# One-hot columns of the key tiles shared between VectorE and ScalarE, and the decode of the sorted list ahead of the last two key products

## What is computed

```python
edge_index = jnp.stack([src, dst])                    # 50000 edges
xn = _layernorm(x, axis=-1)
x = x + gnn(xn, edge_index, w1, b1, w2, b2) \
      + mix(xn[None], Wqkv, bqkv, Wproj, bproj, temperature)[0]
x = x + ffn(_layernorm(x, axis=-1)[None], gate_w, ..., gamma, beta)[0]
# gnn: msgs = mlp(x[col]); agg = segment_sum(msgs, row); mlp(x + agg)
# mix: kn, qn are normalised rows per head (8 heads of 32);
kv_mod = einsum('bhni,bhnj,bhne->bhije', kn, kn, vN)  # all products of two key channels
kv     = einsum('bhnd,bhne->bhde', kn, vN)
```

## Time and profile before

| | us |
|---|---|
| median of 3 runs | 1569.05 |
| lowest, highest | 1567.12, 1572.82 |
| the profiled execution: its time | 1570.75 |
| the profiled execution: its span | 1569.1 |

### The profile page before, as it was taken

How to read it: one execution, slowest core, us unless ns; L and a number is a source line. 1 busy time by engine, 2 the same in 40 slices (tenths; PEclk the granted TensorE clock), 3 DMA queues, 4 the chain that set the end, 5 groups by cost and what they waited for, 6 DMA issues and landing times.

```text
span 1569.1 us, 25750 instructions
## 1 busy us (share of the span) xinstructions
PE 1142.1 (73%) x7084; PEld 777.7 (50%) x7085; DVE 969.9 (62%) x2315; ACT 407.5 (26%) x1088; POOL 953.5 (61%) x1069
## 2 busy tenths in 40 slices
PE   3888869888874776676767776676896399999900
PEld 2656534333332443444444444443685299999900
DVE  4998989999983554445545454454445634343356
ACT  1555321111101322222222222222242032323302
POOL 4597349888876766666666666666100357765416
PEclk8999978898976877788778887787997599999955
DMA  5000000000004444444444454555464222222293
GB/s 152 26 30 30 20 21 1 0 0 0 0 21 135 131 127 130 121 130 125 124 128 128 130 149 125 157 153 128 109 200 152 77 64 70 70 70 70 61 233 101
DMA packets 57119, 145.11 MB, mean 92 GB/s; under 512 B 11117, under 2 KB 24909, under 8 KB 56944
## 3 DMA queue, kind: packets, MB, share of 16 engines
q0 software_dynamic: 33488, 101.80, 22.4%
q1 hardware_dynamic: 23584, 42.74, 9.5%
HBM read 124.91 MB, written 19.59 MB: 92 GB/s over the span
## 4 chain that ended last, share of the span: by engine, by line
PE 45%; DVE 18%; another core or an unknown queue 11%; issue 10%; POOL 5%; DMA 3%; DVEq 3%; ACT 2%; SPq 1%; POOLq 0%; ACTq 0%
PE bank L1766 8%; PE bank L2018 7%; PE bank L2029 7%; DVE big L1162 3%; PE bank L1711 3%; DVE node_buf L1232 3%; DVE big L1163 2%; PE bank L1639 2%; POOL big L635 2%; PE bank L1727 2%; PE bank L1819 2%; PE bank L1827 2%; PE bank L1932 2%; DMA x_buf<-x 1%
## 5 line engine op out<-in xcount | busy, mean ns | idle before, releaser
L713 POOL DMA_INDIRECT big<-msg_rows,big x416 | 420.1, 1010 | 213.3 <-issue 103.8
L1232 DVE TENSOR_TENSOR node_buf<-node_buf,bank 125x256 f32 x416 | 174.6, 420 | 308.2 <-remote 135.3
L1766 PE MATMUL bank<-big 128*128 128x256 bf16 x1248 | 215.1, 321 | 74.5 <-issue 42.0
L1766 PEld LDWEIGHTS bank<-big 128*128 128x128 bf16 x1248 | 130.1, 113 | 151.8 <-issue 67.3
L1162 DVE TENSOR_SCALAR big<-bank,big 125x416 bf16<-125x416 f16 x400 | 192.8, 482 | 7.3 <-PE bank L1639 7.3
L692 POOL TENSOR_TENSOR big<-big 125x512 f32<-125x512 f32 x150 | 170.5, 1171 | 32.6 <-PE bank L1711 30.4
L924 ACT ACTIVATE big<-bank 128x500 f32<-128x500 f32 (+1 forms) x208 | 109.7, 571 | 225.4 <-remote 136.6
L1639 PE MATMUL bank<-big 125*128 125x416 bf16 x400 | 110.5, 363 | 33.5 <-DVE big L1163 31.9
L1163 DVE TENSOR_SCALAR big<-bank,big 125x128 f16<-125x128 f16 x400 | 132.7, 332 | 0.0
L1018 ACT ACTIVATE mid<-bank,const 128x128 f32<-128x128 f32 x256 | 73.2, 368 | 207.0 <-PE bank L2018 188.7
L2029 PE MATMUL bank<-big,mid 128*128 x512 | 121.0, 380 | 0.0
(11 more groups left out here) (303 smaller groups left out, 2067.8 us busy)
## 6 DMA issues: line engine op xcount, KB each, us to landing
big<-L_ffn_w SPq DMA_DIRECT2D x32, 512.0 KB
big<-msg_rows,big POOLq DMA_INDIRECT x416
big<-moe_rows SPq DMA_DIRECT2D x10, 560.0 KB
msg_rows<-big SPq DMA_DIRECT2D x25, 187.5 KB
xn_rows<-mid POOLq DMA_DIRECT2D x5, 625.0 KB, 6.1
x_buf<-x SPq DMA_DIRECT2D x5, 560.0 KB
big<-xn_rows SPq DMA_DIRECT2D x5, 560.0 KB
out<-big SPq DMA_DIRECT2D x5, 560.0 KB
```

The source lines that it names most:

```text
L713: pool.indirect_dma_start(msgs[k], None, msg_rows, bass.IndirectOffsetOnAxis(idx_ring[:, half, k:k + 1], 0)).then_inc(msgs_in[k], 16)
L1232: dve.tensor_tensor(rows, rows, agg_ps[2 * half + j][0:P, :], ALU.add).then_inc(s.agg_add, 1)
L1766: last = mm(agg_ps[k % 4], hot_src[:, turn, k, :], msgs[slot][:, D * i:D * i + D], start=i == 0, stop=i == 2, skip_group_check=True)
```

## The change

Three edits, in words:

1. In tiles 0 to 23, `hot_d` of every third column (c = 2, 5, 8, 11) is built on ACT: `Square(iota - slot_r)` into a small tile `col_gap`, then `Relu(val - val * gap)` into the ring's `hot_d` (`value_columns`, four pairs of instructions after the four of the key tile). PE waits for `col_val_ok` as well at these columns. DVE still builds their `hot_q`, and in the others it builds `hot_d` first and `hot_q` second. The value must be positive for this, so `encode()` moves a sign from `val_dst` into `pow_loc`.
2. ACT needs `-slot_r` and `-val_dst`: one more DVE instruction each (`neg_val` in `encode()`, `neg_slot_r` ahead of the first column), in the space of `src_i` and `dst_i`; `past_end` moves to a space of its own.
3. The decode (`sorted_list`) moves on DVE ahead of the two pair products of tile 24.

```diff
@@ -132,6 +132,9 @@
+        self.col_gap_ok = sem("col_gap_ok")
+        self.col_val_ok = sem("col_val_ok")
+        self.sort_key_ok = sem("sort_key_ok")
@@ -372,7 +375,6 @@
-        past_end = big[0:NB, phase:phase + NQ]
@@ -380,6 +382,10 @@
+        col_gap = [b.take([128], F16, parts=P) for _ in range(2)]
+        past_end = b.take([NQ], parts=NB)
+        neg_slot_r = src_i.bitcast(F32)
+        neg_val = dst_i.bitcast(F32)
@@ -876,9 +882,33 @@
                     act.wait_ge(s.diag_mm, t)
                 act.activation(k_sq, k_v_rows[:, turn, :, 0:128], ACT.Square).then_inc(s.k_sq_ok, 1)
+            def value_columns(t, turn):
+
+                def value(n):
+                    c = 3 * n + 2
+                    act.wait_ge(s.col_gap_ok, t * 4 + n + 1)
+                    act.activation(col_hot[(EARLY + PER * turn + c) % 8][1], col_gap[n % 2], ACT.Relu,
+                                   scale=neg_val[:, bass.ds(t * PER + EARLY + c, 1)],
+                                   bias=val_dst[:, bass.ds(t * PER + EARLY + c, 1)]).then_inc(s.col_val_ok, 1)
+
+                for n in range(4):
+                    c = 3 * n + 2
+                    act.wait_ge(s.col_mm, t * PER + EARLY + c - 7)
+                    if n >= 2 or not at(t, (0,)):
+                        act.wait_ge(s.col_val_ok, t * 4 + n - 1)
+                    act.activation(col_gap[n % 2], iota_r[0:P, :], ACT.Square,
+                                   bias=neg_slot_r[:, bass.ds(t * PER + EARLY + c, 1)]).then_inc(s.col_gap_ok, 1)
+                    if n:
+                        value(n - 1)
+                value(3)
+
             def k_tile(t, turn):
                 k_rows(t, turn)
                 k_squares(t, turn)
+                if not at(t, (T - 1,)):
+                    value_columns(t, turn)
+
+            act.wait_ge(s.sort_key_ok, 1)
             act.wait_ge(s.sort_rows_ok, 4)
             key_tiles(act, k_tile)
@@ -1087,10 +1117,11 @@
                 step(dve.tensor_tensor(rest, dst_i, high, ALU.subtract))
                 chain.add(dve.tensor_scalar(high, high, -2.0 / 2048.0, 1.0, ALU.mult, ALU.add))
                 step(dve.tensor_scalar(even, rest, 1024.0, None, ALU.is_ge))
+                chain.add(dve.tensor_tensor(pow_loc, pow_loc, high, ALU.mult))
                 step(dve.scalar_tensor_tensor(frac, even, -1024.0, rest, ALU.mult, ALU.add))
-                chain.add(dve.scalar_tensor_tensor(rest, even, 1.0, high, ALU.add, ALU.mult))
                 step(dve.tensor_scalar(frac, frac, 1.0 / 1024.0, 1.0, ALU.mult, ALU.add))
-                step(dve.tensor_tensor(val_dst, frac, rest, ALU.mult))
+                step(dve.scalar_tensor_tensor(val_dst, even, 1.0, frac, ALU.add, ALU.mult))
+                step(dve.tensor_scalar(neg_val, val_dst, -1.0, None, ALU.mult))
             moments(0, G)
             inverse(0, G, 1)
@@ -1152,15 +1183,18 @@
             step(dve.tensor_scalar(slot_q, slot_q, MAGIC, None, ALU.add))
             step(dve.tensor_scalar(slot_q, slot_q, MAGIC, None, ALU.subtract))
             step(dve.scalar_tensor_tensor(slot_r, slot_q, -float(SLOT), pos, ALU.mult, ALU.add))
-
-            def columns(first, ring, count):
+            dve.tensor_scalar(neg_slot_r, slot_r, -1.0, None, ALU.mult).then_inc(s.sort_key_ok, 1)
+
+            def columns(first, ring, count, share=False):
                 for c in range(count):
                     hot_q, hot_d = col_hot[(ring + c) % 8]
                     col = lambda a: a[:, bass.ds(first + c, 1)]
                     if not (isinstance(first, int) and first + c < 8):
                         dve.wait_ge(s.col_mm, first + c - 7)
-                    dve.tensor_scalar(hot_q, iota_ps[0:P, :], col(slot_q), col(pow_loc), ALU.is_equal, ALU.mult)
-                    dve.tensor_scalar(hot_d, iota_ps[0:P, 0:128], col(slot_r), col(val_dst), ALU.is_equal, ALU.mult).then_inc(s.col_hot_ok, 1)
+                    if not (share and c % 3 == 2):
+                        dve.tensor_scalar(hot_d, iota_ps[0:P, 0:128], col(slot_r), col(val_dst), ALU.is_equal, ALU.mult)
+                    dve.tensor_scalar(hot_q, iota_ps[0:P, :], col(slot_q), col(pow_loc), ALU.is_equal,
+                                      ALU.mult).then_inc(s.col_hot_ok, 1)
             def norms(lo, hi, n):
                 dve.wait_ge(s.norm_root, n)
@@ -1189,24 +1223,27 @@
                                   kd[:, turn, 6 + j, 0:DH].unsqueeze(1).broadcast_to([P, 16, DH]),
                                   windows(kd_ps[turn][:, j, 1:DH + 1], 16, 1), ALU.mult).then_inc(s.pairs_too_ok, 1)
+            def sorted_list():
+                dve.wait_ge(s.col_mm, EC)
+                step(dve.tensor_scalar(slot_bits, sort_ps.bitcast(I32), 13, None, ALU.logical_shift_right))
+                dve.tensor_scalar(slot_low, slot_bits, 1023, None, ALU.bitwise_and)
+                dve.tensor_scalar(slot_high, slot_bits, 18, 11, ALU.logical_shift_right, ALU.logical_shift_left)
+                dve.tensor_scalar(slot_odd, slot_bits, 10, 1, ALU.logical_shift_right, ALU.bitwise_and)
+                step(dve.tensor_scalar(slot_exp, slot_bits, 10, 255, ALU.logical_shift_right, ALU.bitwise_and))
+                chain.add(dve.scalar_tensor_tensor(slot_low, slot_low, 1024.0, slot_high, ALU.add, ALU.add))
+                step(dve.scalar_tensor_tensor(slot_pair, slot_exp, 1.0, slot_odd, ALU.mult, ALU.add))
+                dve.scalar_tensor_tensor(edge_idx, slot_odd, -1024.0, slot_low, ALU.mult, ALU.add)
+                dve.tensor_scalar(edge_loc, slot_pair, 0.5, -1.0, ALU.mult, ALU.add).then_inc(s.sorted_ok, 1)
+
             def k_tile(t, turn):
+                if at(t, (T - 1,)):
+                    sorted_list()
                 for j in range(2):
                     if not at(t, (T - 1,)):
-                        columns(t * PER + EARLY + PER // 2 * j, EARLY + PER * turn + PER // 2 * j, PER // 2)
+                        columns(t * PER + EARLY + PER // 2 * j, EARLY + PER * turn + PER // 2 * j, PER // 2, True)
                     pair_product(t, turn, j)
             key_tiles(dve, k_tile)
...
@@ -1631,10 +1668,12 @@
                     last = pe.transpose(bview(0, 2, P)[:, k, :], rows[:, 128 * k:128 * k + 128], ident[0:P, 0:P])
                 last.then_inc(s.xnT_mm, 1)
-            def columns(first, ring, count):
+            def columns(first, ring, count, shared={}):
                 for c in range(count):
                     hot_q, hot_d = col_hot[(ring + c) % 8]
                     pe.wait_ge(s.col_hot_ok, first + c + 1)
+                    if c in shared:
+                        pe.wait_ge(s.col_val_ok, shared[c])
                     group = dict(start=at(first, (0,)) and c == 0, stop=at(first, (EC - count,)) and c == count - 1)
                     mm(sort_ps, hot_d, hot_q, skip_group_check=True, **group).then_inc(s.col_mm, 1)
@@ -1719,7 +1758,7 @@
                 def some_columns(n):
                     if not last_one:
-                        columns(t * PER + EARLY + 3 * n, EARLY + PER * turn + 3 * n, 3)
+                        columns(t * PER + EARLY + 3 * n, EARLY + PER * turn + 3 * n, 3, {2: t * 4 + n + 1})
                 pe.wait_ge(s.k_row_ok, t + 1)
                 pe.wait_ge(s.v_row_ok, t + 1)
```

More of the change, by code:

```diff
@@ L1192, in k_tile @@
             def k_tile(t, turn):
+                if at(t, (T - 1,)):
+                    sorted_list()
                 for j in range(2):
                     if not at(t, (T - 1,)):
-                        columns(t * PER + EARLY + PER // 2 * j, EARLY + PER * turn + PER // 2 * j, PER // 2)
+                        columns(t * PER + EARLY + PER // 2 * j, EARLY + PER * turn + PER // 2 * j, PER // 2, True)
                     pair_product(t, turn, j)
             key_tiles(dve, k_tile)
-            dve.wait_ge(s.col_mm, EC)
@@ L1201, in _ @@
-            step(dve.tensor_scalar(slot_bits, sort_ps.bitcast(I32), 13, None, ALU.logical_shift_right))
-            dve.tensor_scalar(slot_low, slot_bits, 1023, None, ALU.bitwise_and)
-            dve.tensor_scalar(slot_high, slot_bits, 18, 11, ALU.logical_shift_right, ALU.logical_shift_left)
-            dve.tensor_scalar(slot_odd, slot_bits, 10, 1, ALU.logical_shift_right, ALU.bitwise_and)
-            step(dve.tensor_scalar(slot_exp, slot_bits, 10, 255, ALU.logical_shift_right, ALU.bitwise_and))
@@ L1206, in _ @@
-            chain.add(dve.scalar_tensor_tensor(slot_low, slot_low, 1024.0, slot_high, ALU.add, ALU.add))
-            step(dve.scalar_tensor_tensor(slot_pair, slot_exp, 1.0, slot_odd, ALU.mult, ALU.add))
-            dve.scalar_tensor_tensor(edge_idx, slot_odd, -1024.0, slot_low, ALU.mult, ALU.add)
-            dve.tensor_scalar(edge_loc, slot_pair, 0.5, -1.0, ALU.mult, ALU.add).then_inc(s.sorted_ok, 1)
             def hot_batch(n, turn):
```

## The result

| us | before | changed |
|---|---|---|
| median | 1570.37 | 1545.76 |
| lowest, highest | 1567.12, 1572.82 | 1542.04, 1549.4 |
| span of the profiled execution | 1569.1 | 1544.5 |

The ratio is 0.984, with a 95% interval of 0.9819 to 0.9862: 24.6 us faster, where 24.0 us were forecast. It lies in the wide range (1541 to 1557.5 us), which takes in three of the rivals, and also in the narrow one (1541 to 1549 us), which does not.

The account below looks back on a forecast made before the run. DVE was taken to set the key tiles' pace. Shared columns -24.5, stalls +1.5, extra instructions +0.6 and decode -1.6 sum to -24.0 us: 1545.0 us from the median 1569.05. Range 1541 to 1557.5 us, forecast case 1541 to 1549.

Parts of the forecast that it names:

- three of the rivals: POOL becoming the bound (1554 us, chance 0.20), issue bounding the columns (1554.6 us, 0.08), gathers taking gain back (1557 us, 0.06).
- The main term: Key tiles: four 128-wide one-hots leave DVE in each of 24 tiles, 1.02 us a tile, saving 24.5 us.
- The issue rival: Key tiles: issue bounds columns without a 128-wide one-hot at some 0.50 us, saving 14.9 us there; 1554.6 us, chance 0.08.
- Stalls of 1.5 us: Key tiles: cold first tile costs DVE up to 0.9 us, low-clock stretches 0.6 us; bounds 0 and 10.
- the floor of 430.2: Key tiles: end of POOL's products at its own pace of 7.91 us a tile, without one further wait.
- The rival that POOL's waits add 9 us: Key tiles: low-clock waits no longer made good, three keeping 3 us each; gain about 15 us, 1554 us, chance 0.20.
- Extra instructions, +0.6 us: One more 400-wide DVE instruction in `encode()` lies on the path: +0.6 us, bounds 0.3 and 1.0; `neg_slot_r` hidden.
- Decode, -1.6 us: After the key tiles: list ready 8.6 to 9.6 us after DVE's last product, 1.6 us gained for gathers, bounds 0 and 3.
- ACT hidden: Key tiles: eight added ACT instructions, 2.9 us, make 4.2 of 8.04 us a tile; added waits taken at 0.
- One of my signs of being wrong: Key tiles: the forecast is wrong if PE's column matmuls are released by ACT.
- Slower: Key tiles: PE runs long stretches at 1.2 GHz and becomes the bound; +20 us, 1589 us, chance 0.04.
- gathers taking the gain back: Gather stage: its own ring and PE's waits take back half the gain; 1557 us, chance 0.06.

Follow-up runs that it names:

- the share of six: Changed kernel with six of twelve columns shared (odd c) instead of four: 1473.55 us against 1498.2 for the kernel before, ratio 0.9839.
- half-product variant: Changed kernel with six columns shared and POOL's products 4 and 5 of each tile at half width: 1464.48 us, once, beside 1474.17 for the changed kernel.
- decode alone: Kernel before with the decode moved ahead of the two products of tile 24, nothing shared: 1567.76 us against 1569.68, ratio 0.9984.
- bits in PSUM: Changed kernel with the decode's first result in a free PSUM bank: 1472.35 us against 1498.2 for the kernel before, ratio 0.9838.

## Why the prediction was right, step by step

- **The main term held.** 24.5 us from a step of 0.41 us for a lone 416-wide one-hot: measured 0.405. DVE's last product of tile 23 moved from 449.97 to 425.75 us, 24.2 us. The tiles with two and with four shared columns give one price per column. The issue rival (0.50 us) is refuted.
- **Stalls of 1.5 us: too high.** The part for the first, cold tile came: DVE waits 0.8 us once, there, against the 0.9 allowed. The 0.6 us for low-clock stretches did not: I carried the low-clock tiles of before over, and none came after the first tile. I had also read the clock of before too kindly: "1.00 in most tiles" is 1.00 in seven of 24. DVE's path had some 1.0 us of stalls before as well (1.8 us idle less 0.8 us behind the last product), so on balance this term is about nothing. POOL's last product ends at 424.11 + 7.21 = 431.32 us, 1.1 us behind the floor of 430.2. The rival that POOL's waits add 9 us fell with the same fact (5.1 us of idle time before its products), though it was right that POOL would be the next bound: the share of six and its half-product variant show that.
- **Extra instructions, +0.6 us:** about 0.7 us at the normalised rows, as forecast. That they lie on the path to the key tiles is not shown: the starts of the first column scatter more than that from trace to trace, and the whole time does not move.
- **Decode, -1.6 us: this step failed.** It set "10.7 us after 449.97" against 8.6 to 9.6, and the 10.7 hold DVE's wait of 2.49 us from a low-clock stretch. At full clock the wait is 1.34 us, and with shared columns the late decode is done 8.17 us after the last product and the early one after 7.86 (with tiles of 9.06 us, 9.36 and 8.87). So the move makes the list 0.3 us earlier (0.5), not 1.6. That the first gather does come 1.6 us earlier (434.5 against 436.1) is luck: it is POOL's two copies, of which the prediction says nothing. "DVE resumes 0 to 1 us earlier: nothing lost" was wrong for the same reason: DVE and PE come out 0.7 to 0.8 us later. The time shows neither: 0.9842 against 0.9844.
- **ACT hidden:** right at four columns. The Square took 0.395 and the Relu 0.479 us against the 0.367 of the row, 3.0 us added busy against 2.9, but a pair 0.98 us in a row of them. One of my signs of being wrong did show: PE's column matmuls were released by ACT 23 times (6.3 us in all, their weight loads 22 times, 15.1 us). It cost nothing, since DVE waited for the ring only once (0.8 us) and one more ACT instruction changed nothing. The ring is also a column deeper than I said: `wait_ge(s.col_mm, first + c - 7)` asks for the product eight columns back, not seven, which leaves ACT 0.65 us more.
- **Slower, and gathers taking the gain back:** the clock went up, not down, and 26.0 us at DVE's one-hot batch became 24.6 at the end. The 1.4 us between are within the runs' scatter.

The sum of 24.0 against 24.6 us thus hides errors of opposite sign: 1.6 us of gain for the decode that its move does not give, and 1.5 us of stalls that on balance were not added. That they cancel is luck; the main term is not. An error of a microsecond or two lies below what the whole times can tell, so this account rests on the traces.

The rule on the shared ports (the Trainium skill, SBUF — State Buffer, "Who interferes with whom") was borne out also for the form that no row of before showed: beside POOL's products, instructions with two SBUF inputs took 1.15 to 1.55 us instead of 0.59 (decode alone, bits in PSUM, and all three of them with six shared columns), and `tensor_scalar` reading PSUM took 0.58 us. In the changed kernel itself the three came after POOL's products (end at 431.32 us, the first of the three at 431.59) and stayed at 0.59 us, so the decode took 7.3 us there and not the 10.7 that the prediction worked out by this rule; with six columns it took 9.6 us.

## What to carry to other kernels

Take work off the engine that the windows show busy without a gap, price it at its step from start to start, and work out the pace of the next engine before sharing more: here 1.02 us a tile was to be had (9.06 to 8.04), and 0.14 us beyond (to 7.90). Count the waits between a helper's own dependent instructions as part of its load; they made 0.98 us of a pair that takes 0.78 where neighbours overlap. Check what stands between an event and its effect before you credit a gain: here two copies moved the first gather by more than the list did. A wait measured where the clock is low says little on the same wait once it is high.

## What had not been expected of the hardware

With tiles of 9.06 us the granted clock was 1.00 in only seven of 24 tiles and fell to 0.54 to 0.59 in four; with tiles of 8.54, 8.0, 7.9, 8.3 and 7.5 us it stayed at 1.00 once the first tiles were past. In all of them PE has more column products in the same time than before. That this is the cause was not isolated: no run changed PE's work at a fixed tile. What the low clock had cost before was small, since DVE stood idle only 1.8 us of 217.4, and then 2.49 us ahead of the last two products.

What ran beside an instruction changed its time more than threefold: POOL's copies of 128x128 and 128x16 took 0.28 and 0.19 us beside DVE's products, whose second input is in PSUM, and 0.95 and 1.19 us beside its one-hot batch, in all of seven and four traces looked at.

The same program took 72 us less on two other chips, all of it in the stage of the gathers. In the windows from 500 to 1000 us of the changed kernel the granted clock is 0.77 to 0.85 on the one and 0.89 to 0.93 on another, and POOL is busy 333 against 373 us. Which is the cause and which follows was not looked into.
